# The second half of the first x behind the first weight block on SyncE's queue, and weight blocks 3 to 7 of batch 0 split one output block later

## What is computed

```
y   = x[b] @ weight[id[b]].T                      # 1024 x 1024, one of 8 weights
base = y @ W_up.T                                 # 1024 x 1024
e   = argmax(y @ gate_w.T + expert_bias)          # one of 4 experts, per token
out[b] = x[b] + base + lora_B[e] @ (lora_A[e] @ y)   # rank 8, scale 1
```

## Time and profile before

| | |
|---|---|
| Time, median of 3 runs | 389.05 us (388.99 to 389.36) |
| The profiled execution: its time | 389.27 us |
| its span in the trace | 387.5 us |
| TensorE busy | 381.2 us (98% of the span) |
| VectorE busy | 212.2 us (55%) |
| ScalarE busy | 144.9 us (37%) |
| DMA, mean over the span | 164 GB/s, 63.70 MB |

### The profile page before, as it was taken

How to read it: one execution, slowest core, us unless ns; L and a number is a source line. 1 busy time by engine, 2 the same in 40 slices (tenths; PEclk the granted TensorE clock), 3 DMA queues, 4 the chain that set the end, 5 groups by cost and what they waited for, 6 DMA issues and landing times.

```text
span 387.5 us, 6808 instructions
## 1 busy us (share of the span) xinstructions
PE 381.2 (98%) x2258; PEld 356.3 (92%) x2258; DVE 212.2 (55%) x493; ACT 144.9 (37%) x318; POOL 1.7 (0%) x11
## 2 busy tenths in 40 slices
PE   7999999999999999999999999999999999999996
PEld 5789998899988999889998999989998899988996
DVE  4776976463564554735737347455365562664132
ACT  5666905370063701536025440345204461054000
POOL 0000000000000000000000000000000000000000
PEclk9999999999999999999999999999999999999999
DMA  7999459702775118643096332872338703540002
GB/s 244 355 415 292 175 208 297 255 7 102 188 251 210 67 41 246 236 167 108 31 277 201 140 108 75 260 247 68 108 123 262 250 15 108 184 141 0 0 0 110
DMA packets 18921, 63.70 MB, mean 164 GB/s; under 512 B 2272, under 2 KB 3424, under 8 KB 18912
## 3 DMA queue, kind: packets, MB, share of 16 engines
q1 hardware_dynamic: 18624, 62.55, 48.2%
q10 hardware_dynamic: 288, 1.05, 0.8%
HBM read 55.20 MB, written 8.39 MB: 164 GB/s over the span
## 4 chain that ended last, share of the span: by engine, by line
PE 95%; DMA 2%; SPq 1%; DVE 1%; issue 0%; ACT 0%; DVEq 0%; ACTq 0%
PE ps_o L485 34%; PE ps_y L474 30%; PE ps_o L494 15%; PE ps_y L476 15%; PE ps_o L509 2%; DMA w_raw<-w_dram 2%; SPq L154 1%; DVE w_lo L352 1%; SPq L164 0%; PE ps_y L502 0%; ACT w_hi L271 0%; DVE rows L400 0%; DVE y_full L408 0%; DVEq L350 0%; ACTq L268 0%
## 5 line engine op out<-in xcount | busy, mean ns | idle before, releaser
L474 PE MATMUL ps_y<-x_hilo,w_hi 128*128 128x512 f32 x512 | 178.8, 395 | 1.2 <-DVE y_full L408 0.6
L476 PE MATMUL ps_y<-x_hilo,w_lo 128*128 128x256 f32 x512 | 142.3, 278 | 0.0
L474 PEld LDWEIGHTS ps_y<-x_hilo,w_hi 128*128 128x128 f32 x512 | 96.0, 188 | 24.3 <-DVE w_lo L345 1.0
L476 PEld LDWEIGHTS ps_y<-x_hilo,w_lo 128*128 128x128 f32 x512 | 96.3, 188 | 0.0
L352 DVE TENSOR_TENSOR w_lo<-w_raw,w_hi 128x512 fp32r<-128x512 f32 x126 | 80.1, 687 | 7.6 <-ACT w_hi L271 7.2
L485 PE MATMUL ps_o<-up_hi,y_hi 128*128 128x366 f32 x256 | 75.0, 334 | 0.0
L485 PE MATMUL ps_o<-up_lo,y_hi 128*128 128x366 f32 x256 | 74.1, 330 | 0.0
L485 PE MATMUL ps_o<-up_hi,y_lo 128*128 128x366 f32 x256 | 74.0, 330 | 0.0
L271 ACT CAST w_hi<-w_raw 128x512 fp32r<-128x512 f32 x126 | 69.9, 620 | 4.8 <-DMA w_raw<-w_dram 4.7
L292 ACT COPY y_small<-ps_y 128x256 f32<-128x256 f32 x64 | 23.9, 373 | 114.4 <-PE ps_y L476 114.4
L408 DVE TENSOR_TENSOR y_full<-ps_y,y_small 128x256 f32<-128x256 f32 x64 | 27.1, 424 | 64.2 <-ACT y_small L292 64.2
(11 more groups left out here) (38 smaller groups left out, 198.6 us busy)
## 6 DMA issues: line engine op xcount, KB each, us to landing
w_raw<-w_dram SPq DMA_DIRECT2D x64, 512.0 KB, 4.2
rows<-x_dram SPq DMA_DIRECT2D x16, 512.0 KB, 5.2
x_raw<-xT_dram SPq DMA_DIRECT2D x14, 512.0 KB, 8.1
up_raw<-w_up_dram SPq DMA_DIRECT2D x8, 512.0 KB, 9.6
out_dram<-rows SPq DMA_DIRECT2D x8, 512.0 KB, 8.6
out_dram<-rows SPq DMA_DIRECT2D x8, 329.0 KB, 7.9
out_dram<-rows SPq DMA_DIRECT2D x8, 183.0 KB, 7.0
x_raw<-xT_dram ACTq DMA_DIRECT2D x2, 512.0 KB, 4.3
```

Of the source, the lines that this page charges most:

```text
L474: pe.matmul(ps_y[c % 2][:, :], w_hi[:, c % RING, cols], x_hilo[:, k, :], start=(k == 0), stop=False)
L476: last = pe.matmul(ps_y[c % 2][:, S:2 * S], w_lo[:, c % RING, cols], x_hilo[:, k, 0:S], start=False, stop=(k == KC - 1))
```

## The change

It has two parts, in batch 0 alone.

1. The DMA of the second half of the first x (steps 4 to 7) is issued by SyncE directly behind weight block 0, no longer by ScalarE behind the first half. The quarters of x and of weight block 0 are split in the order x 0, x 1, w 0, w 1, x 2, w 2, x 3, w 3.
2. Weight block 3 is split no longer ahead of `batch(0)`, but in its c = 0, and so on: block 3 + c in output block c, for c = 0 to 4. Blocks 1 and 2 are still split ahead. The other batches keep block 4 + c in output block c, for c = 0 to 3.

```diff
--- before.py
+++ after.py
@@ -147,6 +147,10 @@
         block = ctx.enter_context(nc.Block())
 
 
+        def load_first_x(queue, d):
+            ks = slice(d * (KC // XD), (d + 1) * (KC // XD))
+            queue.dma_start(x_raw[:, ks, :], xT[0, :, ks, :]).then_inc(x_raw_in[d], 16)
+
         @block.sync
         def _(sp):
             def adapter(b):
@@ -190,7 +194,9 @@
                     sp.dma_start(out[b, toks, 0:CUT], rows[:, t, 0:CUT]).then_inc(stored[t], 16)
 
             i = adapter(0)
-            for c in range(RING):
+            load_w(0, 0, i)
+            load_first_x(sp, XD - 1)
+            for c in range(1, RING):
                 load_w(0, c, i)
             for c in range(RING, OC):
                 load_w(0, c, i)
@@ -290,7 +296,9 @@
 
                     act.wait_ge(y_done, b * OC + c + 1)
                     act.copy(y_small[:, c % 2, :], ps_y[c % 2][:, S:2 * S]).then_inc(y_small_ready, 1)
-                    if c < OC - RING:
+                    if first and c <= OC - RING:
+                        w_hi_part(b, RING - 1 + c)
+                    if not first and c < OC - RING:
                         w_hi_part(b, RING + c)
                     act.wait_ge(y_full_ready, b * OC + c + 1)
                     act.copy(y_hi[:, c, :], y_full[:, c % 2, :]).then_inc(y_hi_ready, 1)
@@ -313,17 +321,16 @@
                     act.copy(zT[:, t, :], ps_y[t][:, 0:P]).then_inc(zt_ready, 1)
 
 
-            for d in range(XD):
-                ks = slice(d * (KC // XD), (d + 1) * (KC // XD))
-                act.dma_start(x_raw[:, ks, :], xT[0, :, ks, :]).then_inc(x_raw_in[d], 16)
-            for q in range(XQ - 1):
+            for d in range(XD - 1):
+                load_first_x(act, d)
+            for q in range(XQ // 2):
                 x_hi(0, q)
-            for q in range(XQ // 2):
+            for q in range(QUARTERS // 2):
                 first_w_hi(q)
-            x_hi(0, XQ - 1)
-            for q in range(XQ // 2, QUARTERS):
+            for q in range(XQ // 2, XQ):
+                x_hi(0, q)
                 first_w_hi(q)
-            for c in range(1, RING):
+            for c in range(1, RING - 1):
                 w_hi_part(0, c)
             batch(0, first=True)
             with act.Fori(1, B - 1) as b:
@@ -407,7 +414,9 @@
                         dve.wait_ge(y_hi_ready, b * OC + c - 1)
                     dve.tensor_tensor(y_full[:, c % 2, :], ps_y[c % 2][:, 0:S], y_small[:, c % 2, :],
                                       ALU.add).then_inc(y_full_ready, 1)
-                    if c < OC - RING:
+                    if first and c <= OC - RING:
+                        w_lo_part(b, RING - 1 + c)
+                    if not first and c < OC - RING:
                         w_lo_part(b, RING + c)
                     dve.wait_ge(y_hi_ready, b * OC + c + 1)
                     dve.tensor_tensor(y_lo[:, c, :], y_full[:, c % 2, :], y_hi[:, c, :].bitcast(F32),
@@ -437,14 +446,14 @@
             dve.memset(warm_f[:, :], 0.0).then_inc(warm_step, 1)
             dve.wait_ge(warm_step, 1)
             dve.tensor_copy(warm[:, :], warm_f[:, :]).then_inc(warm_ready, 1)
-            for q in range(XQ - 1):
+            for q in range(XQ // 2):
                 x_lo(0, q)
-            for q in range(XQ // 2):
+            for q in range(QUARTERS // 2):
                 first_w_lo(q)
-            x_lo(0, XQ - 1)
-            for q in range(XQ // 2, QUARTERS):
+            for q in range(XQ // 2, XQ):
+                x_lo(0, q)
                 first_w_lo(q)
-            for c in range(1, RING):
+            for c in range(1, RING - 1):
                 w_lo_part(0, c)
             batch(0, first=True)
             with dve.Fori(1, B - 1) as b:
```

## The result

| | before | changed | ratio |
|---|---|---|---|
| median of 7 runs each | 389.27 us (388.59 to 389.4) | 390.95 us (389.98 to 391.19) | 1.0038, 95% interval 1.0025 to 1.005 |
| the profiled execution | 389.27 us | 390.01 us | |
| its span | 387.5 us | 388.2 us | |

The ratio is the recorded one, with its interval; it is not the quotient of the two medians (390.95 / 389.27 = 1.0043). The change makes the kernel slower by 0.25 to 0.5%, and the median lies above the range that was given (up to 390.2). The times of the changed kernel come in two groups, three at 390.0 to 390.2 and four at 390.9 to 391.2; the profiled one is of the first group. The rest was in no trace.

What follows compares the result with a forecast made beforehand. TensorE bounds the kernel. The second half of x lands at 9.25; plus 22.90 the second product starts at 32.15 against 32.22, -0.07 us: 389.20 by the profiled execution, 389.1 against the median, range 388.6 to 390.2.

Steps and rivals of the forecast that it cites:

- Edit 2: Later split of blocks 3 to 7: TensorE's wait for y_full at output block 2 goes, with 0.8 us to spare.
- From L to E: TensorE in batch 0: step 4 at L+1.74, block 0 done at L+3.48, seven blocks of 19.42, so E = L+22.90.
- L: Landing time of the second half of the first x behind weight block 0; taken as 9.25 us, between 9.04 and 10.35.
- E: Start of batch 0's second product on TensorE; forecast at 32.15 us against 32.22 before.
- the gap of 1.49: Gap from weight block 1 to 2 on SyncE's queue, taken for x's second half behind block 0; 2.59 called the outlier.
- what is late next: Step naming batch 0's up splits as the next thing to run late, with 0.2 to 0.4 us of slack.
- The up loop: Batch 0's loop of up_hi, up_lo, y_full, y_hi, 2.99 us per round against TensorE's 2.77; start hung on block 7.
- one transfer of 512 KB later: SyncE's queue: blocks 1 to 7 and the first up blocks each come later by one such transfer.
- Block 7 late: Rival: block 7 costs much over 1.3 us more and the up loop binds; +0.34, 389.4 to 389.6 us; chance 0.09.
- The dip falls on x1: Rival: x's second half takes 2.59 us behind block 0, L = 10.35; +1.03, 390.1 to 390.3 us; chance 0.23.
- The drop of TensorE's clock: Clock falling in TensorE's new gap inside block 0: called not likely, given no size and no chance.
- The rule of the Trainium skill: Fixed 2.0 us plus bytes at 436 GB/s for block 0 and x's second half: L = 8.77, a sum of -0.55.

Runs made afterwards that it cites:

- the up blocks first: The changed kernel with the loads of the four up blocks ahead of weight blocks 4 to 7 instead of behind each: 390.08 us, ratio 1.0023.
- gate load early: The changed kernel with the load of the gate and lora_A columns moved ahead on SyncE's queue, behind up block 1: 389.81 us, ratio 1.0018.
- edit 2 alone: The kernel before with only the later split: 388.58 us, ratio 0.9981; also with each half of x in one piece: 388.18 us, 0.9978.
- edit 1 alone: The changed kernel with the splits where they were before, blocks 1 to 3 ahead of y_small(0): 390.82 us, ratio 1.0040.
- the second trace of the changed kernel: The changed kernel measured again without any alteration: 390.38 us, ratio 1.0036 to the kernel before.

## Why the prediction was wrong

It forecast no change, within 388.6 to 390.2; the kernel got slower by 0.38%, a case that it gave 0.25.

- **What bounds the kernel, and that a change before 32 us reaches the end one for one: right.** From the second product on, every kernel took 355.3, within 0.2.
- **Edit 2: right.** TensorE's wait for y_full at block 2 is gone. Alone the edit gives 0.7 in the median.
- **From L to E: right.** Step 4 at L+1.73 (L+1.74 was forecast), the end of block 0 at L+3.47 (L+3.48), and E = L+22.9 where the gate load was out of the way.
- **The term that was mis-sized is L.** 9.25 was taken; 9.58 to 9.76 was measured, 0.3 to 0.5 more. The prediction took the gap of 1.49 and set 2.59, that of the very place in which x1 would stand, aside as an outlier; x1's own gap in that place is 2.2 to 2.8, in six traces. Nor did block 0 stay at 7.76: it landed near 7.3, as the read of the adapter number was no longer beside x1. Both together: L is 2.4 behind block 0, not 1.5.
- **The step that failed in kind is "what is late next".** The up loop was named as next, with 0.2 to 0.4 of slack, and hung on block 7 alone. It hung on the gate load, which stands behind up block 3 on SyncE's queue. Block 7 was where the prediction had it (24.4, against 24.5 to 24.7). The gate load had landed at 24.7 before and came at 27.0 to 27.4; the prediction never placed it.
- **Placing it one transfer later would not have found this.** 24.7 and 1.3 to 1.5 make 26.0 to 26.2, and gate_hi could start at 26.24 (26.98 less its wait of 0.74). The load came 2.3 later because the queue ran dry; without the dry stretch (the up blocks first) it was 0.7. Block 4's issue waits for the last lo quarter of block 0, which edit 1 had tied to x1: L+2.6, 12.4. Block 3, the last one ahead, landed at 13.5, block 4 only 2.2 behind it. The assumption that everything behind x1 comes "one transfer of 512 KB later" is the one that broke: blocks 1 to 3 came only 0.5 to 0.7 later, block 7 1.2, the gate load 2.3. With this the loop costs 0.3 and 0.8 in two of the three traces, 0.1 in the third, and 0.6 to 1.1 by the medians (the gate load early against the changed kernel). A kernel without it (gate load early) is inside the range at 389.8.
- **The rivals.** "Block 7 late" was this mechanism with the wrong load and a chance of 0.09. "The dip falls on x1" (2.59, an L of up to 10.35) was near in size, 2.4. Whether it was the dip or the spaced rows is settled only so far: with whole pieces x1 comes 1.30 behind block 0 and block 1 is the slow one. The drop of TensorE's clock was put aside as not likely and given no chance. With a gap of 3.0 us it came in the traced execution, and the other three have a mean clock at least as low; in the changed kernel 2 of 16 have that mean.
- **The rule of the Trainium skill** (DMA: Bandwidth & Descriptors, "Anatomy of one DMA — SWDGE (gpsimd) path"; 2.0 us and 436 GB/s, an estimate of 8.77 for L) is not borne out for the rows as they lie. For x1 in one piece the 1.30 behind block 0 is near its 1.2; the 2.2 of block 1 behind it is not.
- **The base.** The median of before went from 389.05 with three runs to 389.27 with seven; the sum in its own measure (389.20) was the better place to stand.

## What to carry to other kernels

When a load is put ahead of others in a queue, write down the new landing of every load behind it, the small ones too, and what its consumer's slack was; the one that decides need not be the one that you were looking at. Look also at which issue waits for work that the moved load now holds back: a queue that runs dry charges everything behind it. And when the price of a transfer is read from gaps between others, the gap of the very place in time where it will stand counts most, however much it looks like an outlier; its layout in memory can move it again.

## What the runs showed of the hardware that was not expected

- A load of 128 rows of 4 KB, 8 KB apart, took 2.2 to 2.9 us behind a weight block in seven traces, in one piece it took 1.3 in one trace. Other pieces of 512 KB took 2.1 to 2.6 in that stretch of time too. Right behind x0, whose rows lie between its own, x1 took only 1.2 (4.69 to 5.9). Why the same rows are fast there isn't settled.
- A gap of 3.0 us in TensorE's work was followed by a granted clock of 0.70 and then 0.50, and it cost 1.6 us on top of the gap. In the traces with gaps of 0.9 to 1.6 us the clock stayed at 1.00; but in 6 of the 58 executions of kernels with such a gap the mean clock is 0.996, as with the 3.0 us.
- A tiny read (the adapter number) beside a large transfer decides when the first weight block is issued: 4.4 with both halves of x on the way, 4.0 with one, 3.65 with both in one piece each, 3.69 with one in one piece.
- Some traces have TensorE's steps of the first product 0.353 us apart, others 0.347, through the whole of it and at the same granted clock of 1.00: edit 2 alone (both layouts), edit 1 alone, the up blocks first and the second trace of the changed kernel have the slower one. Over 64 steps it is 0.4 us. What sets it stays open.
